# POOL's state decays moved behind the low parts of the weights, in the first part of a unit

## The reference, cut to what matters

```
proj = einsum('bsd,ed->bse', x, in_proj_w)          # gate, x, B, C, dt
hBC  = silu(causal_conv4(hBC) + conv_b)
dt   = clip(softplus(dt + dt_bias), 0, 100)
...
states     = einsum('bzlhn,bhzl,bzlhp->bzhpn', Bc, decay_states, xch)
new_states = einsum('bhzc,bchpn->bzhpn', decay_chunk, states_p)
Y = Y_diag + einsum(Cc, new_states[:, :-1], exp(A_cum)) + hs * D
g = Y * silu(gate);  out = rmsnorm_by_group(g) * norm_w
x = x + ga * (out @ out_proj_w.T)
```

## Time and profile before

| | |
|---|---|
| median of 3 runs | 1913.36 us (1913.02 to 1916.5) |
| the profiled execution | 1919.0 us, of which its span is 1917.2 us |
| PE busy | 1828.7 us, 95% of the span |
| DVE, ACT, POOL busy | 1294.0, 1061.2 and 938.7 us |
| mean granted TensorE clock | 0.983 |
| POOL L1486 (decays) | 96 times, 1061 ns each |
| POOL L1436 (low parts), wx and wg | 64 and 80 times, 1406 and 1408 ns each |

### The profile page before, as it was taken

The page is one execution under the profiler, slowest core; times in us unless marked ns, Lnnn a source line. Parts: engine busy times, 40 slices in busy tenths (PEclk is TensorE's granted clock), DMA queues, the critical chain, the costliest instruction groups (busy, mean ns, idle before and its releaser), DMA issues.

```text
span 1917.2 us, 31312 instructions
## 1 busy us (share of the span) xinstructions
PE 1828.7 (95%) x9752; PEld 1408.7 (73%) x9752; DVE 1294.0 (67%) x2094; ACT 1061.2 (55%) x1935; POOL 938.7 (49%) x717
## 2 busy tenths in 40 slices
PE   7889999999999999999999999999999999999966
PEld 6767778777777777777777777777777777777745
DVE  4856667666766667666676667666676666766688
ACT  5455555656546565555546565465665555565632
POOL 1225464555435465354645554354654545454564
PEclk9799999999999999999999999999999999999988
DMA  4412121121212121021211112121211212112121
GB/s 173 142 51 70 53 64 48 39 61 52 70 33 64 48 67 50 28 67 58 66 44 45 57 49 70 33 64 48 67 50 30 65 59 64 43 46 61 34 94 55
DMA packets 76393, 114.14 MB, mean 60 GB/s; under 512 B 21696, under 2 KB 27328, under 8 KB 75328
## 3 DMA queue, kind: packets, MB, share of 16 engines
q1 hardware_dynamic: 58656, 80.07, 14.2%
q10 hardware_dynamic: 17568, 31.99, 5.0%
HBM read 88.94 MB, written 23.07 MB: 58 GB/s over the span
## 4 chain that ended last, share of the span: by engine, by line
issue 45%; POOL 33%; PE 12%; DVE 4%; ACT 2%; DMA 1%; SPq 1%; POOLq 1%; ACTq 0%; DVEq 0%
POOL yt L1505 9%; POOL ssq L1500 6%; POOL wg_lo L1436 4%; POOL wo_lo L1436 4%; POOL prev L1486 3%; POOL yt L1508 3%; POOL wx_lo L1436 3%; PE bank L449 3%; PE bank L451 2%; PE bank L450 2%; PE bank L586 1%; PE bank L479 1%; PE bank L734 1%; PE bank L648 1%; PE bank L782 0%
## 5 line engine op out<-in xcount | busy, mean ns | idle before, releaser
L1505 POOL TENSOR_TENSOR yt<-yt,ea 128x384 f32<-128x384 f32 (+1 forms) x128 | 189.9, 1483 | 413.2 <-DVE ea L1352 413.2
L1136 DVE SCALAR_TENSOR_TENSOR xc<-bank,bpar,xc 128x511 f32<-128x511 f32 (+2 forms) x384 | 285.8, 744 | 63.4 <-ACT xc L848 58.9
L1322 DVE TENSOR_TENSOR lm<-lm,cbm 128x512 f32<-128x512 f32 x256 | 186.1, 768 | 164.5 <-ACT lm L993 164.5
L449 PE MATMUL bank<-h_hi,wg_hi 128*128 128x512 f32 x640 | 263.6, 412 | 16.7 <-ACT gate L949 13.9
L451 PE MATMUL bank<-h_hi,wg_lo 128*128 128x512 f32 x640 | 252.0, 394 | 0.0
L450 PE MATMUL bank<-h_lo,wg_hi 128*128 128x512 f32 x640 | 251.7, 393 | 0.0
L449 PE MATMUL bank<-wo_hi,g_hi 128*128 128x512 f32 x496 | 206.8, 417 | 6.1 <-POOL wo_lo L1436 6.1
L449 PE MATMUL bank<-h_hi,wx_hi 128*128 128x512 f32 x512 | 211.3, 413 | 1.1 <-DVE craw L1136 0.7
L1486 POOL TENSOR_TENSOR prev<-prev,dec 128x512 f32<-128x512 f32 x96 | 101.8, 1061 | 220.7 <-DVE prev L1271 132.3
L450 PE MATMUL bank<-h_lo,wx_hi 128*128 128x512 f32 x512 | 201.6, 394 | 0.0
L451 PE MATMUL bank<-h_hi,wx_lo 128*128 128x512 f32 x512 | 201.0, 393 | 0.0
(11 more groups left out here) (182 smaller groups left out, 3866.7 us busy)
## 6 DMA issues: line engine op xcount, KB each, us to landing
raw_w<-w_in_dram SPq DMA_DIRECT2D x145, 256.0 KB, 2.7
raw_w<-w_out_dram SPq DMA_DIRECT2D x64, 256.0 KB, 2.6
part_d<-part ACTq DMA_DIRECT2D x64, 256.0 KB, 2.1
part<-part_d ACTq DMA_DIRECT2D x58, 256.0 KB, 2.7
rt<-rows_d SPq DMA_DIRECT2D x256, 8.0 KB
acc<-x_dram SPq DMA_DIRECT2D x8, 256.0 KB, 6.6
acc<-w_mod_dram SPq DMA_DIRECT2D x2, 1024.0 KB, 6.4
lh<-neg_d SPq DMA_DIRECT2D x128, 8.0 KB
```

The costliest lines, as they stand in the source:

```text
L449: nc.tensor.matmul(out_ap, whi(k), hhi(k), start=(k == 0), stop=False)
L1136: stt(dst[:, at], ps[:, 0:HALF - 3 + k], w(k), dst[:, at], ALU.mult, ALU.add)\
L1322: tt(lm[:, h % 4, :], lm[:, h % 4, :], cbm[:, toks(hf)], ALU.mult).then_inc(v_m, 1)
L1505: tt(yt[:, j % 2, cols], yt[:, j % 2, cols], ea[:, j % 2, cols], ALU.add).then_inc(p_t3, 1)
```

## The change

In the loop over the steps z of a unit's first part, POOL's decay is issued behind the low parts of the same step (and behind the power of the variance) and no longer ahead of them. Nothing else is changed; the other engines' programs are the same.

```
@@ -1477,6 +1477,10 @@
                 todo = by_step(fills(g, c, 0, last))
                 for z in range(NZ):
 
+                    if z == 0 and not first and c in (0, 3):
+                        group_rstd(g - 1 if c == 0 else g, 1 if c == 0 else 0)
+                    for f in todo[z]:
+                        unit_fill(f, g)
                     if z >= 1 - hf and z < NZ - hf:
                         if z == 1 - hf:
                             po.wait_ge(d_par[hf], 224 * (nb + 1))
@@ -1486,10 +1490,6 @@
                         tt(prev[:, slot(hf, z + 1), :].rearrange("p (h c) -> p h c", h=BH),
                            prev[:, slot(hf, z), :].rearrange("p (h c) -> p h c", h=BH),
                            d.unsqueeze(2).broadcast_to((128, BH, HDIM)), ALU.mult).then_inc(p_dec, 1)
-                    if z == 0 and not first and c in (0, 3):
-                        group_rstd(g - 1 if c == 0 else g, 1 if c == 0 else 0)
-                    for f in todo[z]:
-                        unit_fill(f, g)
                 todo = fills(g, c, 1, last)
```

More of the change, by code:

```diff
@@ L1488, in unit @@
                            d.unsqueeze(2).broadcast_to((128, BH, HDIM)), ALU.mult).then_inc(p_dec, 1)
[L1489 to L1492, removed]
                 todo = fills(g, c, 1, last)
```

## The result

| | before | change |
|---|---|---|
| median of 15 runs each | 1914.56 us (1911.96 to 1918.55) | 1909.50 us (1906.56 to 1911.45) |
| profiled execution | 1919.0 us | 1906.93 us |
| its span | 1917.2 us | 1905.1 us |
| mean granted clock | 0.983 | 0.984 |
| PE waits at L734 for L1241 | 7.8 us, 7 times | none |

The ratio of the runs is 0.9969, with a 95% interval of 0.9962 to 0.9976: the change is faster by 0.31%, 5.9 us (4.6 to 7.3); the two medians alone differ by 5.1 us. The median of 1909.50 us is inside the range that was given, and 5.9 us above the forecast, by coincidence the same number. The two profiled executions differ by twice as much as the runs do, 12.1 us, and that gap is the question of what follows.

The account below looks back on a forecast made before the run. PE, busy 95% of the span, bounds the kernel; its L734 waits for a chain through POOL's D1 and C. Waits -5.8 and clock -4.0 sum to -9.8 us, from a 1913.4 us median to 1903.6, range 1900.5 to 1913.5.

Parts of the forecast that it names:

- C by 0.9 us, low part 1.27: c = 3 units on POOL: C's low part, no longer behind D1, takes 1.27 us and is done 0.9 us earlier.
- X1 at 6.6 to 7.4 us behind B's start: c = 3 units on ACT: X1's high part comes 6.6 to 7.4 us after B's low part starts, 8.3 before.
- L734 at 15.0 to 15.2: c = 3 units on PE: the first L734 starts 15.0 to 15.2 us after B's low part starts, 16.0 before.
- waits: PE's waits at L734 in the seven c = 3 units shrink: 5.4 us in six, 0.4 in the first group, -5.8 us.
- The units with c = 1 and SP's queue, 0: Eight c = 1 units, where N0 has 1.9 us of cover, and SP's earlier copies change nothing: 0.
- The last unit, 0: Very last unit: D0 is 1 us late behind the power, ahead of an N0 that comes 2 us later: 0.
- The clock, -4.0: The low clock behind PE's idle time at L734 goes in three c = 3 units, 1.3 us each; bounds 0 and 4.0.
- the step from one execution to the median: The profiled execution is 5.6 us over the median; the same difference is taken off the forecast, giving 1903.6 us.
- the last of the signs that I had named for being wrong: The prediction is wrong if the mean clock stays at its value.
- the first rival: The clock stays: the waits shrink but the half clock comes elsewhere or was rarer in unprofiled runs; 1907.6 us, chance 0.22.
- the second: The gain is given back at PE's next wait, above all ACT's gates, or through late N2; 1911 to 1914 us, chance 0.15.
- Slower by X0 and D1: c = 3 units: late X0 copy delays D1, N1 and PE's L586 one for one; 1916 to 1918 us, chance 0.08.

Follow-up runs that it names:

- e1: The kernel before, unchanged, traced a second time: ratio 1.0 (0.9991 to 1.001), profiled at 1917.2 us.
- e3: The kernel before with the new POOL order in the units with c = 1 alone: ratio 0.9997 (0.9988 to 1.0006).
- e6: The kernel before with the new POOL order in the very last unit only: ratio 1.0003 (0.9993 to 1.0012).
- e10: The kernel before, unchanged, traced a third time: profiled at 1917.4 us.
- e2: The kernel before with the new POOL order only in the seven c = 3 units that have low parts: ratio 0.9964 (0.9951 to 0.9977).
- e4: The kernel before with only C's low part put ahead of D1 in the seven c = 3 units: 1905.57 us, ratio 0.9955 (0.9942 to 0.9968).
- e9: The kernel before with ACT's second load of `part` in c = 3 units issued behind X1's high part: 1909.27 us, ratio 0.9965 (0.9951 to 0.9978).
- e7: The kernel before with an unused 1.0 us POOL operation ahead of C's low part in the seven c = 3 units: ratio 1.0033 (1.0022 to 1.0044).
- e8: The changed kernel with an unused 1.0 us POOL operation between X0's low part and D1: 1914.93 us, ratio 1.001 (1.0001 to 1.0018) against before.

## Why the prediction was right, and by what it was off

**The chain: right.** N0, D1, C, X1's copy, ACT, masks, L1241, L734 is what held PE, as the c = 3 version, the version with C alone and the version with the load moved show from three sides.

**C by 0.9 us, low part 1.27: right** (0.92, and 1.29 us).

**X1 at 6.6 to 7.4 us behind B's start: missed on the good side**, 6.25. The copy was 1.1 us shorter as well: with 0.17 us from C's end to its issue, as before, it took 708.00 - 705.29 - 0.17 = 2.5 us, less than the short one of my two bounds (2.8, from X0).

**L734 at 15.0 to 15.2: 14.84**, and 14.7 to 14.9 in the seven units. It is 1.2 us earlier in this unit (1.1 in the mean of the six) and not 0.9. The new wait at L586 that I had put at 0.2 us a unit isn't there in any of the seven: X0 came 0.2 us sooner than before (7.08 us behind the power, 7.31 before), and D1 and N1 with it. The 0.3 us that L586 waits more in all belong to the last unit. So the term "waits" was too small: 7.8 us gone in this pair of traces, 7.4 in the mean of the five traces of the old order, instead of 5.8.

**The units with c = 1 and SP's queue, 0: right** (stretches of 155.0 us, ratio 0.9997).

**The last unit, 0: wrong.** "D0 is 1 us late, ahead of an N0 that comes 2 us later" looked at the order and not at what D0 now stands beside. It costs 0.6 us.

**The copy's spread: missed.** In 0 of 7, 2 of 7 and 1 of 7 units of the three traces of the change X1 came late and PE waited 0.5 to 0.6 us. By that count it is some 0.5 us a run.

**The clock, -4.0, and the step from one execution to the median: this is what failed.** The mechanism is in the traces: of the 35 c = 3 units in five traces of the old order (before, `e1`, `e3`, `e6`, `e10`) 12 have the half clock behind the wait, all of them among the 31 waits of 0.76 us and more; of the 42 where that wait is gone or under 0.7 us (three traces of the change, `e2`, `e4`, `e9`) none has. And the difference of the profiled executions, mean of five against mean of three, is 1917.3 - 1908.7 = 8.6 us. But the runs that are timed give 5.9, and their mean granted clock is 0.983 for both kernels (61 runs of the kernel before beside the experiments, 20 of the change), the last of the signs that I had named for being wrong. With 7.4 for the waits, less 0.6 for the last unit and 0.5 for the copy, some 6 us are left, which is the whole measured gain.

Counted another way, the seven L734 start 131.8 us behind their powers in sum with the old order (mean of five traces) and 125.9 with the change (three): 5.9 us earlier, and 5.3 when the last unit's cost is taken off. With `e2`, `e4` and `e9` they start 6.0, 7.6 and 5.8 us earlier, and the timed runs gained 6.9, 8.6 and 6.7. So the timed runs leave about 1 us for the clock and not 4 (the interval is 1.4 us either way for the change, some 2.5 for the other three).

All five of the profiled executions with the old order at c = 3 are over the median of the timed runs, 1914.6, as the first was by 5.6 us over 1913.4. I had seen that difference and taken it for a constant, to be subtracted from both sides; that is the step that failed.

By its size the clock can account for most of the gap. Of those 61 timed runs the six at a mean clock of 0.981 took 1915.5 to 1920.2 us and the eleven at 0.985 or 0.986 took 1911.1 to 1913.2, about 1 us for a thousandth over all 61. The five profiled executions with the old order have 0.982 in the mean and the three of the change 0.984, two thousandths apart where the timed runs have none, beside the 2.7 us between 8.6 and 5.9. So the executions that were profiled fell on the low side of the clock in the one order and on the high side in the other. That this was chance is not shown: the timed runs don't tell their clock by unit. `e7` speaks against a rule, since it was profiled at 1918.0 us, 2.5 under its own median. This stays open.

The result, 1909.5, lies between the first rival (the clock stays, 1907.6) and the second (the gain is given back, 1911 to 1914). The first describes the timed runs best. Of the 1.9 us above it 1.2 are the base: the median of the kernel before was 1913.36 in 3 runs and 1914.56 in 15. The misses in the waits largely cancel, 1.6 us more gained and 1.1 lost in the last unit and by late copies. That the time fell inside the range with most of the clock term missing is owed to that and to a range of 13 us.

**Slower by X0 and D1: it didn't happen, but was near.** 1.0 us is enough for it.

## What to carry to other kernels

Where a queue feeds both a transfer and a state update, put ahead only what frees the transfer: moving C alone did at least as much as moving three decays, and in its trace left no new edge. Before moving an operation, look at which transfer its successor's copy meets and which instruction of the neighbour engine it will lie beside; a load issued 3 us later, out of the way of a copy, was worth as much as the whole reordering. And take a gain in clock from one profiled execution only as far as that execution agrees with the timed runs.

## What the runs showed of the hardware that I had not expected

- A 128x512 load of X1 issued 0.2 us behind a load of `part` from the other queue was in ACT's hands 3.65 us later. With that neighbour a microsecond or more ahead (`e7`) it took 2.7 to 3.0, with the neighbour moved behind X1 (`e9`) 2.4 to 2.7. With the neighbour 0.7 us behind it, as in the change, it was 2.4 to 3.1 us in 28 of 35 units and 3.4 to 4.0 in seven (three traces of the change, `e2` and `e8`).
- Where POOL's decay and DVE's two-input L1241 meet, it was the one that started second that paid, and the more, the more of the first was left: L1241 took 1.49 us in place of 0.75 where the decay had begun 0.12 us ahead of it (last unit of the change), 1.06 where it had begun 0.6 us ahead and about 0.9 at 0.7 us, and the decay kept its 1.06. The decay took 1.51 where L1241 had begun first, as with C moved alone, and L1241 then 0.81. The 1.73 of C is the same: L1241 had begun 0.46 us ahead of it.
- A stand of PE of 0.76 to 1.5 us was followed by the 1.2 GHz level 12 times in 31, in units that changed from one execution of the same kernel to the next. The four waits under 0.5 us in the same traces were not followed by it.
